# Two attentions of a recurrent two-layer kernel rebuilt: transposed expert down projection, and 32-query blocks with half transposes

## The reference

```python
# layer 0, "first attention": gated linear attention, 16 heads of 16
gk = log_sigmoid(x @ Wgk1 @ Wgk2 + bgk2) / 16
def step(state, inp):                       # over the tokens
    state = state * exp(gt)[..., None] + vt[..., None] * kt[..., None, :]
    return state, einsum('bhvk,bhk->bhv', state, qt)
out = layernorm(out) * gamma + beta
s = (out * silu(x @ Wg)) @ Wout
# layer 0, feed-forward: 8 experts, the best two of each token, bottleneck 64
h = relu(einsum('td,edb->teb', xf, Wd) + bd)
y = 0.5 * (einsum('teb,ebd->ted', h, Wu) + bu)
f = einsum('te,ted->td', gates, y)          # gates: softmax over the two best
# layer 1, "window attention": 16 query heads, 2 key heads of 16, 64 keys a query
scores = einsum('bgrsd,bgswd->bgrsw', qg, k_win)    # keys s-32 .. s+31
out = einsum('bgrsw,bgswd->bgrsd', softmax(scores), v_win)
s = out @ Wo + bo
# layer 1, feed-forward: ternary weights, hidden 1024
h = bitlinear(x, w_fc) + gate * (x @ v.T @ fast_b.T @ u.T)
f = bitlinear(relu(h) ** 2, w_proj)
```

## Time and profile before

| | |
|---|---|
| median of the runs | 3878.38 us |
| the profiled execution | 3877.76 us, span 3876.0 us |
| TensorE (PE) matmul busy | 3650.6 us, 94% |
| VectorE (DVE) busy | 2777.5 us, 72% |
| ScalarE (ACT) busy | 1962.9 us, 51% |
| GpSimd (POOL) busy | 1082.2 us, 28% |
| granted TensorE clock | 0.996 of full speed |

### The profile page before, as it was taken

One profiled execution on the slowest core, in us unless ns is written; L12 is line 12 of the kernel. 1 busy time (PEld: TensorE's weight loads), 2 busy tenths in 40 slices (PEclk: granted clock), 3 DMA queues, 4 the chain that ended last, 5 costly groups with the idle time before them and its releaser, 6 DMA issues. The chain is left out here.

```text
span 3876.0 us, 73403 instructions
## 1 busy us (share of the span) xinstructions
PE 3650.6 (94%) x26748; PEld 2384.1 (62%) x26748; DVE 2777.5 (72%) x6223; ACT 1962.9 (51%) x4311; POOL 1082.2 (28%) x1313
## 2 busy tenths in 40 slices
PE   3999999999999999999989999999999999999999
PEld 2666566665666656566655666656666566665656
DVE  4767777777667767677666776777767766777767
ACT  2264562745536365373644726446274553636536
POOL 2323233231322313223122232323323232231322
PEclk9999999999999999999999999999999999999999
DMA  3000010000000000000000100001000010000000
GB/s 85 1 12 23 1 34 1 13 21 8 27 1 18 17 12 23 1 30 5 12 23 1 33 2 12 23 1 34 1 14 21 2 33 1 16 19 12 23 1 23
DMA packets 72652, 62.28 MB, mean 16 GB/s; under 512 B 18032, under 2 KB 71904, under 8 KB 72288
## 3 DMA queue, kind: packets, MB, share of 16 engines
q1 hardware_dynamic: 72288, 57.52, 4.9%
HBM read 40.72 MB, written 16.78 MB: 15 GB/s over the span
## 5 line engine op out<-in xcount | busy, mean ns | idle before, releaser
L786 POOL TENSOR_TENSOR qx<-qx 128x512 f32<-128x512 f32 x256 | 281.1, 1102 | 760.6 <-ACT qx L1003 760.6
L1251 DVE TENSOR_REDUCE row_max<-bank 128x4 f32<-128x512 f32 x512 | 339.2, 684 | 137.6 <-PE bank L1585 134.4
L1139 DVE TENSOR_TENSOR am<-bank,causal 128x512 f32<-128x512 f32 x512 | 317.2, 682 | 17.5 <-PE bank L1443 17.5
L1329 DVE TENSOR_TENSOR sq_lo<-qx,sq_hi 128x512 fp32r<-128x512 f32 x256 | 205.5, 803 | 155.0 <-ACT sq_hi L982 154.5
L1598 PE MATMUL bank<-ident,am 128*128 128x128 f32 x2048 | 297.1, 278 | 14.2 <-ACT qx L938 9.4
L1598 PEld LDWEIGHTS bank<-ident,am 128*128 128x128 f32 x2048 | 230.6, 141 | 92.1 <-issue 48.9
L1258 DVE TENSOR_TENSOR am<-bank,row_max 128x512 f32<-128x512 f32 x384 | 265.6, 692 | 14.6 <-PE bank L1598 1.1
L723 POOL TENSOR_SCALAR o_veps<-o_mom 128x1 f32<-128x1 f32 x128 | 28.5, 223 | 881.6 <-DVE o_mom L1209 879.3
L922 ACT ACTIVATE am<-am 128x512 f32<-128x512 f32 x384 | 261.1, 680 | 5.5 <-DVE am L1258 5.5
L1363 PE MATMUL bank<-w_down,xt 128*128 128x512 f32 x512 | 252.2, 615 | 0.0
L1520 PE MATMUL bank<-w_up,hgt 128*128 128x256 f32 x1024 | 246.2, 381 | 3.7 <-ACT hgt L878 3.7
(11 more groups left out here) (252 smaller groups left out, 8933.0 us busy)
## 6 DMA issues: line engine op xcount, KB each, us to landing
qt<-in_L_attn_x SPq DMA_DIRECT2D x136, 128.0 KB, 2.2
x<-in_L_attn_x SPq DMA_DIRECT2D x128, 128.0 KB, 2.3
out<-x SPq DMA_DIRECT2D x128, 128.0 KB, 1.7
x<-in_L_ffn_w_fc SPq DMA_DIRECT2D x1, 1024.0 KB, 5.7
attn<-in_L_ffn_w_proj SPq DMA_DIRECT2D x1, 1024.0 KB, 7.7
w_up<-in_L_ffn_Wu SPq DMA_DIRECT2D x1, 512.0 KB, 6.0
w_down<-in_L_ffn_Wd SPq DMA_DIRECT2D x2, 256.0 KB, 3.7
w_vg<-in_L_attn_Wv SPq DMA_DIRECT2D x1, 256.0 KB, 4.4
```

The lines of the kernel that those rows point to most:

```text
L786: nc.gpsimd.tensor_tensor(sq[:, n % 3, :], relu[:, n % 3, :], relu[:, n % 3, :], ALU.mult)\
L1139: nc.vector.tensor_tensor(am_tiles[:, :, j], bank[3 + j][:].rearrange("p (f e t) -> p f e t", f=2, e=2), causal[:].unsqueeze(1).unsqueeze( ...
L1251: nc.vector.tensor_reduce(row_max[:, j, :], scored, AX.X, ALU.max, negate=(j == 0))\
L1329: nc.vector.tensor_tensor(sq_lo[:, n % 3, :], sq[:, n % 3, :], sq_hi[:, n % 3, :].bitcast(F32), ALU.subtract)\
```

## The change

Both attentions are rebuilt at once.

First attention and experts: the down projection is made with the hidden units on partitions and 512 tokens a matmul (`experts_down`), so that its result needs no transposes. ScalarE takes bias and relu from the bank. The gate of each token must then lie on all partitions of its expert: the gates are transposed (L1474 after), copied to `gate_rows`, written to memory by a DMA, and read back to `g_wide` spread over partitions (two DMAs of 512 KB for each half of the tokens). GpSimd multiplies (`hidden_gated`). Four of the eight down projections are made in the head and one at the end of each of chunks 0 to 3. In a chunk the scores come first, the up projection comes before `cumulate`, and both state products come before the narrow products. VectorE masks three score tiles before it takes the values. Parts of the second normalisation are made in earlier chunks, and tokens are transposed two chunks at a time (`pair_turn`).

Window attention: the block is 32 queries (`WB`) with 96 keys (`KW`). The mask uses four row groups, the scores tiles of 32 rows and 32 columns. A transpose takes 64 queries of one head (64 rows, 96 columns), and the two halves of the partitions go to two banks. `probs_turn(c, p)` does 16 of them. The first half of the probabilities of a chunk is turned before the next scores, the second behind them, and the values of a chunk follow in the same step.

The core of the diff:

```diff
-KW = 192
+WB = 32
+KW = WB + WIN
...
+for g in range(NG):
+    sp.wait_ge(s["gx_ok"], at("gx_ok", g + 1))
+    sp.dma_start(gate_dram[g], gate_rows[8:8 + E, g * 512:(g + 1) * 512]).then_inc(s["gw_ok"], 16)
+    sp.wait_ge(s["gw_ok"], at("gw_ok", 16 * (g + 1)))
+    if g:
+        sp.wait_ge(s["hm_ok"], at("hm_ok", 4))
+    for e in range(2):
+        rows = gate_dram[g].rearrange("(j e) t -> e j t", e=2)[e]
+        sp.dma_start(g_wide[e * BN:(e + 1) * BN], rows.partition_broadcast(BN)).then_inc(s["gl_ok"], 16)
...
+def hidden_gated(c):
+    g, cols = c // 4, slice(c % 4 * P, (c % 4 + 1) * P)
+    pool.wait_ge(s["hr_ok"], at("hr_ok", 4 * (g + 1)))
+    pool.wait_ge(s["gl_ok"], at("gl_ok", 32 * (g + 1)))
+    nc.gpsimd.tensor_tensor(hidden_t[g][:, :, cols], hidden_t[g][:, :, cols], g_wide[:, :, cols], ALU.mult)\
+      .then_inc(s["hm_ok"], 1)
...
+def experts_relu(i):
+    g, j = i // 4, i % 4
+    act.wait_ge(s["hp_ok"], at("hp_ok", i + 1))
+    if i == 4:
+        act.wait_ge(s["gkl_ok"], at("gkl_ok", NC // 2))
+    nc.scalar.activation(hidden_t[g][:, j, :], bank[5 if g else j][:], ACT.Relu, bias=b_down[:, j:j + 1])\
+      .then_inc(s["hr_ok"], 1)
...
+experts_relu(0)
+experts_relu(1)
+first_queries_keys(4)
+first_queries_keys(5)
+experts_relu(2)
+experts_relu(3)
+for b in range(NG):
+    act.wait_ge(s["gtp_ok"], at("gtp_ok", b + 1))
+    nc.scalar.copy(gate_rows[:, b * 512:(b + 1) * 512], bank[gate_banks[b]][32:64, :]).then_inc(s["gx_ok"], 1)
...
-    for j in range(4):
+middle_state(0)
+for c in range(NC):
+    for j in range(3):
         causal_scores(c, j)
+    dve.wait_ge(s["tg_ok"], at("tg_ok", c + 1))
+    decayed_values(c)
+    causal_scores(c, 3)
+    output_gate(c)
...
+def experts_down(i):
+    g, j = i // 4, i % 4
...
+for k in range(KD):
+    mm = nc.tensor.matmul(bank[5 if g else j][:], w_down[:, k, j * P:(j + 1) * P],
+                          xt[:, k, g * 512:(g + 1) * 512], start=(k == 0), stop=(k == KD - 1))
+mm.then_inc(s["hp_ok"], 1)
...
+experts_down(0)
+experts_down(1)
+first_queries_keys(4)
+first_queries_keys(5)
+experts_down(2)
+experts_down(3)
+pe.wait_ge(s["gates_ok"], at("gates_ok", 7))
+for b in range(NG):
+    pe.wait_ge(s["hr_ok"], at("hr_ok", 2 - b))
+    for j in range(4):
+        mm = nc.tensor.transpose(bank[gate_banks[b]][:, j * P:(j + 1) * P], gates[:, 4 * b + j, :], ident[:])
+    mm.then_inc(s["gtp_ok"], 1)
+first_queries_keys(6)
+first_queries_keys(7)
...
-    pe.wait_ge(s["f1_ok"], at("f1_ok", c))
-else:
+if c == 0:
     pe.wait_ge(s["qk_ok"], at("qk_ok", 6))
+elif c <= 4:
+    pe.wait_ge(s["hr_ok"], at("hr_ok", 4 + c))
...
-    parity_scores(c)
-    pe.wait_ge(s["hgt_ok"], at("hgt_ok", c))
-    token_major(bank[2][:], c, w_down).then_inc(s["hp_ok"], 1)
-if c + 1 < NC:
+    experts_up(c, 0)
+    experts_up(c, 1)
     cumulate(c + 1)
+else:
+    pe.wait_ge(s["f1_ok"], at("f1_ok", c))
+    pair_turn(0)
+    pe.wait_ge(s["ktok_ok"], at("ktok_ok", c))
+    pe.wait_ge(s["f2_ok"], at("f2_ok", c - 1))
+    pair_turn(1)
 pe.wait_ge(s["am_ok"], at("am_ok", 4 * c + 4))
-if c == 0:
-    pe.wait_ge(s["gt_ok"], at("gt_ok", 2))
...
 for half in range(2):
     nc.tensor.matmul(bank[7][:, half * P:(half + 1) * P], state_mid[:, half, :],
-                     qt[:, half, c * P:(c + 1) * P], start=True, stop=False,
+                     qt[:, half, c * P:(c + 1) * P], start=(half == 0), stop=False,
                      skip_group_check=True)
+for half in range(2):
...
+    if c < 4:
+        experts_down(4 + c)
+    attention_token_major(c)
+experts_up(NC - 1, 1)
 def queries_keys(n):
...
-rows = slice(j % 2 * QB, (j % 2 + 1) * QB)
-nc.tensor.matmul(bank[1 + j][:], twice_bf[rows, :],
-                 band_q[rows, :].unsqueeze(1).broadcast_to([QB, 4, P]),
+rows = slice(j * WB, (j + 1) * WB)
+nc.tensor.matmul(bank[1 + j][:, 0:4 * KW], four_bf[rows, :],
+                 band_q[rows, :].unsqueeze(1).broadcast_to([WB, 4, KW]),
...
-for b in range(2):
+for b in range(4):
...
-first = c * P + b * QB
-mm = nc.tensor.matmul(bank[1 + j][b * QB:(b + 1) * QB, t * 2 * P:(t + 1) * 2 * P],
-                      q2[rows, t, first:first + QB], k2[rows, :, first:first + P],
+first = c * P + b * WB
+mm = nc.tensor.matmul(bank[1 + j][b * WB:(b + 1) * WB, t * 2 * KW:(t + 1) * 2 * KW],
+                      q2[rows, t, first:first + WB], k2[rows, :, first:first + KW],
...
+def probs_turn(c, p):
+    pe.wait_ge(s["pr_ok"], at("pr_ok", 4 * c + 2 * p + 2))
+    if c or p:
+        pe.wait_ge(s["pt_ok"], at("pt_ok", 4 * c + 2 * p))
+    for h in range(8):
+        for r in range(2):
+            rows = slice(r * QB, (r + 1) * QB)
+            mm = nc.tensor.transpose(bank[5 + r][0:KW, h * QB:(h + 1) * QB],
+                                     pr[rows, 2 * p + h // 4, h % 4, :], ident[rows, rows])
+            if h == 7:
+                mm.then_inc(s["ptp_ok"], 1)
...
+probs_turn(0, 0)
+window_values(0)
+window_values(1)
+for c in range(NC - 1):
+    score_masks(c + 1)
+    score_quad(c + 1)
+    if c:
+        attention_turn(c - 1)
+    probs_turn(c, 1)
+    if c:
+        attention_project(c - 1)
     else:
...
+        window_values(2)
+        window_values(3)
+    values(c)
+    probs_turn(c + 1, 0)
+    values_turn(c)
+hidden(0, 0)
+hidden(0, 1)
+attention_turn(NC - 2)
+probs_turn(NC - 1, 1)
+hidden(1, 0)
+hidden(1, 1)
+attention_project(NC - 2)
 hidden(2, 0)
-attention_turn(NC - 2)
```

409 lines of the change are left out of this document (194 added, 215 removed).

## The result

| | before | after |
|---|---|---|
| median of the runs | 3877.43 us | 3907.82 us (3906.77 to 3912.47, 4 runs) |
| span of the profiled execution | 3876.0 us | 3910.7 us |
| TensorE busy | 3650.6 us | 3493.3 us |
| VectorE busy | 2777.5 us | 2543.2 us |
| GpSimd busy | 1082.2 us | 1267.0 us |

The ratio of after to before is 1.008, with a 95% interval of 1.0063 to 1.0098. The change makes the kernel slower, where 3739 us, 3.6% faster, was forecast. The busy time of TensorE fell by 157 us all the same: the loss is idle time and a lower clock. An upper bound for the clock's part is an estimate from the two means: (0.996 - 0.979) x 3910.7 = about 66 us, as if TensorE had been busy all through.

A forecast was written before the change was run, and what follows sets the result against it. TensorE was taken as the bound in the first attention's steady chunks and as full in the window attention. First attention -1.4 and window attention -7.3 made -8.7 us a sequence, x 16 = -139: 3739 us, range 3650 to 3822.

The forecast's parts named there:

- (a): First attention: the four transposes of hg go, saving 0.65 us of TensorE a chunk.
- chunks 1 to 3: First attention: less TensorE work, but scores wait 0.45 us for the down projection's relu; saved 2.0 us a sequence.
- third rival: Freed TensorE time becomes waits on VectorE and ScalarE: window period 6.3, chunks 4 to 6 at 12; 3823 us, chance 0.15.
- Chunk 7 and the normalisations: Last chunk of the first attention: 2.7 us less work, partly returned as mask waits; 2.3 saved, 0.3 for transposed pairs.
- Chunks 4 to 6: First attention: VectorE's chain sets them at 11.1 us each, 0.7 once for normalisations; saved 3.4 us a sequence.
- The head: Sequence head and chunk 0: more down projections, a 2.4 us decay wait and 0.5 for the gate; +6.6 us.
- rival of the late gate: The gate's way through memory is late: at 5 us 3819 us; chance 0.09, 0.03 of it slower than before.
- Window attention: Chain through ScalarE and TensorE gives a 5.75 us period against 6.54; with start and end, -7.3 us a sequence.
- issue rival: Window attention: small products go by the instruction, scores 2.1 us, each transpose group 1.0; 3951 us, chance 0.08.
- two signs of being wrong: Profile after: a window period above 6.3 us, or a head grown by over 9 us, would show the forecast wrong.

The follow-up runs named there:

- e10: e9 with the gate projection ahead of the scores in chunks 0 to 4 and half a down projection over ScalarE's copy in chunks 1 to 3; 3779.09 us.
- e11: e10 with the up projection of chunk 0 moved behind its masked products; 3754.80 us.
- e6: The kernel after, with VectorE's normalisations for chunks 0 to 3 moved into its gap before the state products of chunk 6; 3856.34 us.
- e12: The kernel after, with useless products in TensorE's waits for VectorE in chunks 6 and 7; 3878.71 us.
- e3: The kernel after, with one useless gate projection between the cumulation and the scores of chunk 0, in the decay wait; 3901.98 us.
- e5: e3 without the expert gate's DMAs and the wait for them; GpSimd multiplies by a constant instead; 3876.92 us.
- e9: e6 with VectorE's addition to x and its two statistics operations moved behind the next chunk's masks; 3821.38 us.
- e1: The kernel before, with only the window attention of the kernel after; 3804.13 us.

## Why the prediction was wrong, step by step

The forecast was -8.7 us a sequence and +2.3 came (235.82 to 238.10 us). By the stretches of the sequence shown the 11.0 us between them are 4.0 in chunk 7 with its way to the window attention, 3.4 in chunks 1 to 6, 2.9 in the window attention and 0.6 in the head. Most of the first two are one error of mechanism: TensorE work was taken off the sum although waits for other engines lay under it.

- **(a), the hg transposes: the step that failed in chunks 1 to 3.** They were worth 0.65 us of work a chunk and it was all counted. But they covered ScalarE's copy of `ot`, and a wait of 0.58 us took their place (65.2 us in 112 waits). With a relu wait of 0.65 where 0.45 was put, chunks 1 to 3 gained nothing (12.46 us; 11.83 was forecast). e10 and e11 took both waits away and reached 11.35. This was the third rival, freed TensorE time that turns into waits, but it was priced for chunks 4 to 6 and the window attention (6.3 us a period; 6.18 came), not for ScalarE's copy in chunks 1 to 3.
- **Chunk 7 and the normalisations: the largest miss.** 2.7 us less work, 0.3 for the pairs and 0.4 back as a wait gave -2.6; +1.4 was measured. TensorE's idle time in the stretch grew from 2.8 to 5.5 us, 2.3 more than put: the waits are 1.69 for `xn`, 2.00 for the masks (1.05 before) and 0.56 for `ot`. The normalisations were priced at 0.7 once; they stand ahead of the masks of chunk 6 (1.05 us) and of chunk 7, and hold up the second pair of transposes. TensorE's busy time fell by only 1.3 us for 3.0, with half clock in it (0.93 over the stretch). Moving the normalisations gave 51 us (e6), part of it clock.
- **The clock: a term that was missing.** Each wait was priced at its length. In after the granted clock falls to half behind the 2.48 us wait of chunk 0 in ten sequences, in chunk 6 in six and in chunk 7 in all. Filling waits with useless work, nothing else changed, gave 29 us in chunks 6 and 7 (e12) and 6 us in the head (e3). By the estimate from the means the clock's part is at most about 66 us of the 169 us between the forecast and the result. e5's 31 us do not count as clock, since e5 also leaves out the gate's DMA.
- **Chunks 4 to 6: right in the sum, by luck in part.** The forecast had VectorE's chain at 34.0 us for the three, 11.1 each and 0.7 once; they took 34.62 (1106.46 to 1141.08), half clock in chunk 6 included, and 33.5 without it. But one by one they are 10.02, 11.22 and 12.28 us: the chain does not set chunk 4, and the normalisations cost chunk 6 more than 0.7. e9 shows the chain in chunks 5 and 6 by shortening it.
- **The head: right by errors that cancel.** +7.15 for +6.6. The half clock added 1.6 us in this sequence; the gate, 0.5 in the sum, cost nothing in the ten slow sequences, 0.8 to 1.2 us in the six others and up to 1.25 once TensorE was faster (e3). Flight 6.0 us, decay wait 2.48 for 2.4. The rival of the late gate did not happen at the size that it named (5 us).
- **Window attention: the chain was right, its terms and the waits were mis-sized.** -4.4 us a sequence for -7.3, 74 us (e1) for 117, 60% of the size. Start and end came within 0.3 us. The period was summed along a chain through ScalarE at 5.75, and that chain sets it, at 6.18: the score products cost 0.31 more than the 0.9 taken, the other terms add up to 0.12 more. No run shortened ScalarE's work alone, so how close behind the chain TensorE's own work lies was not measured. Six periods gained 2.0 us instead of 4.5.
- **The issue rival: wrong.** It needed 2.1 us for the scores and 1.0 for half transposes; 1.21 and 0.58 came. By the Trainium skill ("TensorEngine Tiling (Array Packing)", Instruction Overhead) each matmul carries about 60 cycles, an estimate of 1.6 us for the 64; the runs have 0.90 us with 96 columns and 1.21 with 192, and they decide.

The forecast named two signs of being wrong, a window period above 6.3 us and a head that grows by over 9. Neither came (6.18 and 7.15): it put chunks 1 to 3 at 11.8 us but named no bound for them, and it had no sign at all for chunk 7, where most was lost.

That e11, at 3754.8 us, ends close to the forecast is no merit of the sum: it gets there with five changes of order on VectorE and TensorE that the forecast did not have. What stays open: why only some waits are followed by half clock (the 2.48 us of chunk 0 in ten sequences of after, chunk 6 in six, and not the 2.84 us wait of e6's chunk 7 in five), and how much of e5's 31 us would come without taking the gate's DMA away.
